# Another order of loads, projection quarters, branches and residuals around the fusions, and other banks

## The reference

```python
# layer 0: attention by heads of 8 channels
q, k, v = x @ wq.T, x @ wk.T, x @ wv.T            # per pixel
pw = pointwise(depthwise5x5(concat(q, k, v)))
out = relu_linear_attention(concat(q, k, v, pw))   # 1024 channels
y = proj(out) * inv + (bn_beta - bn_mean * inv)    # batch norm folded
x2 = y + x
# layer 1: edge maps
sobel, lap, diag, grad = four 3x3 gradient maps of x2
feat = gelu(bn(einsum('kbchw,koc->kbohw', E, w_branch) + b_branch))   # 4 x 128 channels
att = sigmoid(gelu(mean(feat) @ w_att1.T + b_att1) @ w_att2.T + b_att2)
z = w_fuse @ (feat * att) + b_fuse
out = gelu(layernorm_over_channels(z) * ln_gamma + ln_beta) + x2
```

## Time and profile before

| | |
|---|---|
| median of 3 runs | 5199.48 us (5190.54 to 5200.01) |
| profiled execution, its own time | 5196.7 us |
| its span | 5194.8 us |
| mean granted TensorE clock | 0.976 |
| PE busy | 4887.5 us, 94% |
| DVE busy | 2583.4 us, 50% |
| ACT busy | 2021.1 us, 39% |
| `edges` begins / its first projection matmul | 3141.4 / 3157.5 us |

### The profile page before, as it was taken

One profiled execution on the slowest core, in us unless ns is written; L12 is line 12 of the kernel. 1 busy time (PEld: TensorE's weight loads), 2 busy tenths in 40 slices (PEclk: granted clock), 3 DMA queues, 4 the chain that ended last, 5 costly groups with the idle time before them and its releaser, 6 DMA issues. The chain is left out here.

```text
span 5194.8 us, 65292 instructions
## 1 busy us (share of the span) xinstructions
PE 4887.5 (94%) x22760; PEld 3445.3 (66%) x22760; DVE 2583.4 (50%) x3635; ACT 2021.1 (39%) x3671; POOL 1223.1 (24%) x1030
## 2 busy tenths in 40 slices
PE   8999999999999999999999996899899989998958
PEld 7887887888888888888888883344344434443423
DVE  3333333333334334424434421786688578847865
ACT  3333333333333333333323320454555455545555
POOL 2342342342342332332332330000300020011003
PEclk9999999999999999999999998999999999999969
DMA  6666665666666666666656644443344344434313
GB/s 188 198 208 202 197 214 199 198 212 205 198 216 202 204 206 206 206 197 215 206 186 225 203 151 168 142 155 112 130 136 150 108 144 130 141 118 135 117 35 115
DMA packets 390811, 893.09 MB, mean 172 GB/s; under 512 B 33488, under 2 KB 66512, under 8 KB 388240
## 3 DMA queue, kind: packets, MB, share of 16 engines
q1 hardware_dynamic: 390544, 889.18, 51.8%
HBM read 588.74 MB, written 300.32 MB: 171 GB/s over the span
## 5 line engine op out<-in xcount | busy, mean ns | idle before, releaser
L733 POOL TENSOR_TENSOR toeplitz<-taps 128x512 f32<-128x512 f32 x768 | 889.1, 1185 | 955.2 <-PE bank L441 955.2
L441 PEld LDWEIGHTS bank<-toeplitz,columns 128*128 128x128 f32 x8192 | 954.4, 192 | 13.9
L441 PE MATMUL bank<-toeplitz,columns 128*128 128x128 f32 x8192 | 955.7, 275 | 0.0
L1029 PE MATMUL bank<-att,w_proj 128*128 128x512 f32 x2048 | 909.6, 598 | 34.1 <-DVE centred L1314 23.8
L1029 PEld LDWEIGHTS bank<-att,w_proj 128*128 128x128 f32 x2048 | 393.0, 192 | 531.8 <-issue 523.3
L356 PE MATMUL bank<-x_hi,w_hi 128*128 128x512 f32 x1536 | 610.9, 398 | 18.4 <-DVE x_lo L600 18.4
L1362 POOL TENSOR_TENSOR centred<-centred,x_out 128x512 f32<-128x512 f32 x128 | 164.5, 1318 | 1937.1 <-ACT centred L1176 1937.1
L358 PE MATMUL bank<-x_lo,w_hi 128*128 128x512 f32 x1536 | 601.2, 391 | 0.0
L357 PE MATMUL bank<-x_hi,w_lo 128*128 128x512 f32 x1536 | 599.7, 390 | 0.0
L1042 PE MATMUL bank<-edge,w_branch 128*128 128x512 f32 x1024 | 494.5, 629 | 96.1 <-ACT edge L1130 96.1
L671 DVE TENSOR_SCALAR ckey_t<-bank 128x256 f32<-128x256 f32 x256 | 107.4, 419 | 881.8 <-PE bank L441 881.4
(11 more groups left out here) (115 smaller groups left out, 5629.8 us busy)
## 6 DMA issues: line engine op xcount, KB each, us to landing
x_sb<-in_x_tiled SPq DMA_DIRECT2D x128, 1024.0 KB, 6.4
tiles_dram<-tiles SPq DMA_DIRECT2D x128, 867.0 KB, 6.8
loaded<-tiles_dram SPq DMA_DIRECT2D x256, 433.5 KB, 4.0
inverse<-inverse_dram SPq DMA_DIRECT2D x256, 256.0 KB, 5.0
att_dram<-out_sb SPq DMA_DIRECT2D x256, 256.0 KB, 4.1
att<-att_dram SPq DMA_DIRECT2D x64, 1024.0 KB, 6.3
xb<-x_dram SPq DMA_DIRECT2D x128, 330.0 KB, 3.2
x_out<-in_x_pad SPq DMA_DIRECT2D x32, 1056.0 KB, 5.5
```

The source lines that it names most:

```text
L441: last = nc.tensor.matmul(bank[:, v * M:(v + 1) * M], columns[:, h % 2, t - T_K, v + b, a * HT:(a + TO) * HT], w[:, t, d, :], start=(d == ...
L733: last = nc.gpsimd.tensor_tensor(toeplitz[:, h % 2, t, :].rearrange("p (d o r) -> p d o r", o=HD, r=PL), tap, point, ALU.mult)
L1029: last = nc.tensor.matmul(P_BANKS[m][:, :], w_proj[:, i * HALF + k, m * P:(m + 1) * P], att[:, i, k, :], start=(i == 0 and k == 0), stop=( ...
```

## The change

In `edges`:

1. SyncE first loads the mixed weights and the first chunk of `att`, then `edge_vec`, then the first residual, and only then the other constants. VectorE's start waits for `edge_vec` alone.
2. What VectorE makes of the other constants (`constants`), and the four tiny matmuls that average `b_fuse` (`bias_mean`), move behind the three steps of projection alone, into `drain(0, None)`; so do ScalarE's waits for them.
3. `drain` on SyncE loads both halves of `att` for chunk 3 before it writes chunk 2 of x2.
4. In a fresh step TensorE runs q0 q1 b0 q2 b1 q3 b2 b3. In a leaving step it runs q0 b0 q1 b1 q2 b2 b3 q3.
5. `P_BANKS` and `Z_BANKS` are reassigned: the last tile of a fusion lies in bank 4, which is now m = 3 of the projection; banks 5, 6, 7 (m = 0, 1, 2) held tiles of chunk 6. The fresh step's wait for `normed` is split: m = 0 to 2 wait for chunk 6's tiles, m = 3 and b0 for the last. `NORMED` is a larger starting count.
6. VectorE adds the residual of the leaving chunk's m = 2, 3 after `pooled`, not before.

```diff
@@ edges(): banks and the offset of normed
-        P_BANKS, VAR_BANK = banks[4:8], banks[0]
-        Z_BANKS = [banks[i] for i in (4, 5, 6, 7, 1, 2, 3)]
+        VAR_BANK, Z_BANKS = banks[0], banks[1:8]
+        P_BANKS = (banks[5], banks[6], banks[7], banks[4])
+        NORMED = START + KT
@@ SyncE, start and step
-                    for dst, src in ((vec[:, :, :].rearrange("p v m -> p (v m)"), io["vec"]),
-                                     (w_branch[:, :, :, :].rearrange("p k e o -> p (k e o)"), io["branchT"]),
+                    for i in range(2):
+                        load_mixed(0, i)
+                        load_att(0, 0, i)
+                    sp.dma_start(vec[:, :, :].rearrange("p v m -> p (v m)"), io["vec"]).then_inc(vec_loaded, 16)
+
+                def load_constants():
+                    for dst, src in ((w_branch[:, :, :, :].rearrange("p k e o -> p (k e o)"), io["branchT"]),
...
-                    for i in range(2):
-                        load_mixed(0, i)
-                        load_att(0, 0, i)
...
                         load_x(*pj, slot)
+                        if mj is None and prev_p is None:
+                            load_constants()
@@ SyncE, drain
                     if p is not None:
-                        write_x2(p, LAG - 1, (LAG - 1) % 2)
                         sp.wait_ge(att_used, chunk(p, LAG))
                         load_att(p, LAG, 0)
                         sp.wait_ge(projected, KT * chunk(p, LAG))
                         load_att(p, LAG, 1)
+                        write_x2(p, LAG - 1, (LAG - 1) % 2)
                         load_rows(p, 0, 0, 16 * chunk(p, LAG))
@@ TensorE: the mean of b_fuse moves from start into bias_mean, into VAR_BANK
+                def bias_mean():
                     pe.wait_ge(ready, 2)
                     for k in range(KT):
-                        last = nc.tensor.matmul(banks[4][:, 0:1], mean_w[:, :], v("b_fuse")[:, k:k + 1],
+                        last = nc.tensor.matmul(VAR_BANK[:, 0:1], mean_w[:, :], v("b_fuse")[:, k:k + 1],
...
                     pe.wait_ge(ready, 5)
@@ TensorE, project and step
                         if i == 0:
                             pe.wait_ge(summed, KT * c + m + 1)
+                            if fresh:
+                                pe.wait_ge(normed, NORMED + KT * chunk(p, 0) - (KT if m < KT - 1 else 0))
...
-                    if fresh:
-                        pe.wait_ge(normed, START + KT * chunk(pj[0], 0))
-                        pe.wait_ge(std_ready, START + chunk(pj[0], 0))
-                    for k in range(KT):
-                        if pj is not None:
-                            project(*pj, k)
-                        if mj is not None:
-                            branch(*mj, k)
+                    leaving = pj is not None and mj is not None and isinstance(pj[1], int) and pj[1] == LAG - 1
+                    for k in range(KT + 1):
+                        if pj is not None and k < KT and not (leaving and k == KT - 1):
+                            project(*pj, k, fresh)
+                        if mj is not None and k - fresh in range(KT):
+                            if fresh and k == 1:
+                                pe.wait_ge(normed, NORMED + KT * chunk(pj[0], 0))
+                                pe.wait_ge(std_ready, START + chunk(pj[0], 0))
+                            branch(*mj, k - fresh)
+                    if leaving:
+                        project(*pj, KT - 1, False)
 
                 def drain(p, b):
-                    pass
+                    if b is None:
+                        bias_mean()
@@ ScalarE: its waits for scaled and ready move from start to drain(0, None)
-                    act.wait_ge(scaled, 3)
-                    act.wait_ge(ready, 5)
...
@@ VectorE, start: waits for edge_vec alone; the rest of the constants moves
-                    dve.wait_ge(const_loaded, 96)
+                    dve.wait_ge(vec_loaded, 16)
...
+                    dve.wait_ge(scaled, 3)
+
+                def constants():
+                    dve.wait_ge(const_loaded, 80)
                     nc.vector.tensor_scalar(bn_scale[:, :], v("bn1_gamma"), float((1.0 + EPS_BN) ** -0.5), None,
...
@@ VectorE, drain and fusion
                 def drain(p, b):
-                    if p is not None:
+                    if b is None:
                         add_residual(p, LAG - 1, (LAG - 1) % 2, (2, 3))
+                        constants()
...
                     nc.vector.tensor_scalar(pooled[:, :], row_sum[:, :], 1.0 / N, None, ALU.mult).then_inc(pooled_ready, 1)
+                    if not last_image:
+                        add_residual(b + 1, LAG - 1, (LAG - 1) % 2, (2, 3))
                     dve.wait_ge(gate_ready, KT * (b + 1))
```

More of the change, by code:

```diff
@@ L1015, in start, with project @@
                     pe.wait_ge(ready, 5)
-                def project(p, j, quarter):
+                def project(p, j, quarter, fresh):
                     c = chunk(p, j)
@@ L1154, in drain @@
                 def drain(p, b):
-                    if b is not None:
+                    if b is None:
+                        act.wait_ge(scaled, 3)
+                        act.wait_ge(ready, 5)
+                    else:
                         features(b, NCH - 1)
@@ L1229, in start @@
                     dve.wait_ge(mean_ready, 1)
-                    nc.vector.tensor_scalar(z_shift[:, :], v("b_fuse"), banks[4][:, 0:1], None, ALU.subtract).then_inc(ready, 1)
+                    nc.vector.tensor_scalar(z_shift[:, :], v("b_fuse"), VAR_BANK[:, 0:1], None, ALU.subtract).then_inc(ready, 1)
                     nc.vector.tensor_reduce(row_sum[:, :], w_fuse[:, :, :], AX_X, ALU.add).then_inc(ready, 1)
```

12 lines of the change are left out of this document (7 added, 5 removed).

## The result

| | before | changed |
|---|---|---|
| median, in the same session | 5199.48 us (5 runs) | 5169.13 us (5166.08 to 5172.72, 5 runs) |
| ratio | | 0.9948, 95% interval 0.9935 to 0.9961 |
| span of the profiled execution | 5194.8 us | 5164.3 us |
| from attention's last matmul to the end | 2081.2 us | 2054.6 us |

The kernel is 30.3 us faster by the medians; 41.2 had been forecast.

A forecast was written before the change was run, and what follows sets the result against it. PE was taken to set the pace (busy 94%), so only its idle or half-clock time could be saved. Terms 8.0 + 0.3 + 20.4 - 1.5 + 14.0 = 41.2 us off 5196.7 gave 5155; forecast 5147 to 5163, 8-in-10 range 5142 to 5176.

The forecast's parts named there:

- The start: First loads: issuing PE's two loads ahead of the constants starts projection earlier, 8.0 us saved (7.0 to 9.0).
- After the projection-only steps: Before the first b0: the first map decides, not the 8.81 us wait for att; 0.3 us saved (-2.6 to +2.3).
- The leaving step: Three transitions: q3 covers the 3.66 us wait, plus 1.0 us less half clock; 4.7 us each, 14.0 in all.
- b3 of a leaving step: Sign against the forecast: a 4 us wait for maps there would take away what q3 covers.
- The fresh step: Four fresh steps: one quarter less from b0 to next b0, partly lost to a wait; 5.1 us each, 20.4 in all.
- wait of 2.9 us: Before the b0 following a fresh step: VectorE's chain leaves this wait in place of 0.93 us.
- The half clock: Fresh b0 after the fusion, three times: longer idleness costs 0.5 us each (0 to 1), -1.5 us in the sum.
- the freed banks: After the fusion: q0 and q1 run at once, but b0 still comes with its map, so the 8.02 us bring nothing.
- The 11 us of wait before b0: Sign in images two to four: PE's idleness after the fusion falls in one piece before the fresh b0.
- (a): Rival: VectorE paces the shortened steps, so the fresh steps bring nothing; 20.8 us saved, 5176; chance 0.12.
- (b): Rival: the start isn't held by the queue order, so its 8.0 us go; 5163.5; chance 0.08.
- (d): Rival: PE stays at half clock through each fresh step after idleness, 22.3 us a step, 89 for four; 5245; chance 0.03.

The follow-up runs named there:

- start_old: Changed kernel with SyncE's first loads in the order of before; 43.5 us from attention's end to first projection (changed 36.6), 2058.3 us after attention (changed 2054.6).
- leaving_old: Changed kernel with the leaving step's q3 back ahead of b3 and VectorE's residual back ahead of pooled; 2067.6 us after attention, 13.0 longer.
- residual_late: Changed kernel with VectorE's residual for the previous chunk's m = 2, 3 behind the second input tile's maps; 2055.7 us after attention against 2054.6.
- fresh_old: Changed kernel with the fresh step back in order q0 b0 q1 b1 q2 b2 q3 b3; median 5175.99 us, ratio to before 0.9964.
- wait_late: Changed kernel, new banks kept, but a fresh step's q0 and q1 wait for all norms of the fusion before; median 5162.05 us, ratio 0.9932.
- banks_old: Changed kernel with the banks of before, so a fresh step's q0 waits for the last norm; 2041.0 us after attention, 13.5 less.
- ahead_all: Changed kernel with order q0 q1 b0 q2 b1 q3 b2 b3 in every paired step but the leaving one; median 5147.67 us, ratio 0.9911.

## Why the prediction was right or wrong

The direction and the range (5142 to 5176) held, and so did the sizes of the start and of the leaving step; 5155 was 14 us too low. After attention the gain was 26.6 us where the sum has 41.2. The range held partly by luck: its upper end was kept for VectorE setting the pace, which did not happen, and the time that came instead is half clock. Another 3.8 of the 30.5 us between the two profiled executions lie in `attention`, which the change doesn't touch.

- **The start**, 8.0 us: 7.3 in the trace, 6.9 of it by start_old from the order of the loads. PE began 8.2 us after the first issue (3138.14 to 3146.38 in this trace), I had 7.9.
- **After the projection-only steps**, 0.3 us: -1.0 in the trace (111.1 for 110.2). About 0.5 of it lies in the 192 matmuls ahead (85.57 us for 85.06), the rest behind T; among the kernels with the same order the figure varies by 1.5 us. The reading, that the first map decides and the 8.81 us don't count, held, and so did both estimates of what the queue would do (2.6 us lost by the write, 2.1 regained by the rows).
- **The leaving step**, 14.0 us: 13.1 in the trace, 13.0 by leaving_old. The 3.66 us each were right. The half clock gave back 2.1 us in all for 3.0, and not in the fusion's first 40 matmuls, where I had put it (in the first image 19.87 us for 19.24), but in the small matmuls ahead of them. No b3 of a leaving step waited.
- **The fresh step**, 20.4 us: 17.1 from b0 to b0 (4.3, 3.9, 4.7 and 4.3 for 5.1). Taken without b0's own time it is 4.3 us in every image (38.7 before, 34.4 changed): the quarter of 6.87 less the growth of the wait from 0.93 to 3.49. The step that failed is "But VectorE's work ahead of that b0 gets no shorter ... Behind it come the map itself, ScalarE's absolute, the table load and two roots". I took VectorE's chain through the residual to the diagonal map as the one that ends last. It is ScalarE's, through `features`, which can't start before the maps of input 0 are done; residual_late moved the residual and moved nothing. The kernel before could have told: by my chain its b0 would have come at 3308.3 (the diagonal map's 3304.30 and 4.0 us), and it came at 3311.99. What the chain leaves out is one table load and four gelus. The size came near by luck, since the two chains end within 1 us of each other in the changed order. (With its own wait of 2.9 us for 0.93 the term would have been 4.9.)
- **The half clock**, 1.5 us: this was the largest error, 6.7 us. The part that I priced came out smaller than priced: 0.5 us of loss for each fresh b0 of images two to four, measured 0.1 us for the three together (6.30, 5.40 and 6.53 us for 5.92, 5.74 and 6.48). The step that failed is the "wait of 2.9 us" that the fresh step leaves, priced at 2.9 us and nothing for the clock. At 3.5 us it was followed by a b0 at 6.4 to 6.6 us in three images of the changed kernel, 2.7 us each, 8.2 us in all; fresh_old, with 0.93 us of wait, has 3.70 us in all four.

The terms as measured are 7.3 - 1.0 + 17.1 + 13.1 - 8.2 = 28.3. Of the 1.7 us to the 26.6, 1.6 lie in the last image, whose first two branches without projection took 6.32 and 6.29 us for 5.58 and 5.40.

What the prediction missed beside its sum is what the early q0 and q1 forgo. That the freed banks as such bring nothing (V to E0 26.2 us in every kernel) was right; that letting PE run early is at worst a small loss was wrong. In the kernel before q0 came after 8.0 us of idleness and took the half clock on itself, with time to spare. With two quarters in a row that would have carried PE to b0 without a pause: wait_late and banks_old, in which PE starts later, gain 11.4 and 13.5 us over the change. The 11 us of wait before b0 in images two to four came in the last image alone (11.46). In images two and three q0 itself began 5.2 us late, and 3.6 and 4.1 us were left before b0.

Of the rivals, (a) did not happen: in an order that leaves no wait before b0 VectorE still kept pace (ahead_all). (b) fell with start_old. (d) had the right mechanism in miniature: half clock at the branches after idleness, for one branch and not a step. The rule drawn from the Trainium skill, page "ScalarE: Activation LUTs", section "Rules for kernel authors", about 2.7 us per switch of table set, is not what the trace shows: from the end of the activation ahead of a switch to the start of the one behind it there are 1.30 us (3289.90 to 3291.20 above), 1.28 of them the load. The Trainium skill's page "TensorE: Matmul & The Clock Gate", section "HAM oscillation — how this bites in real kernels", says that a matmul kernel which waits between bursts pays the transition to half clock again and again. The slow fresh b0 after 3.25 us of wait and more, in every kernel here, agrees with it; the next b0 after its 3.48 us was slow in some images and not in others. Here the payment falls on whatever PE runs first afterwards, which may or may not be on the path: on q0 and q1 in wait_late, on b0 in the changed kernel.

## What to carry to other kernels

Before freeing an engine to start early, ask what it will wait for next: if that is fixed by others, the early work only moves the idle time, and idle time of PE directly ahead of work on the critical path can cost that work its clock (for a branch here after waits of 3.25 us and more, never after 1.7 us and less). Better idle first, run slow where there is slack, and arrive without a pause. Where a step of cover is taken away before a matmul, follow every engine's queue back from it, not the busiest one's, and then give the cover in pieces as long as the chains need: two quarters or three tiles before b0 and one or two tiles between the others, together with the later start, was worth 28 us over the change by the medians of two sessions, 31 us in the part after attention.

## What the runs showed of the hardware

- A wait of 3.48 us before the b0 that follows a fresh step had different consequences in like places: the matmuls after it took 3.70 us (changed kernel, first image; banks_old, first and last image; and others), 5.40 us, or 6.4 to 6.6 us. Waits of 0.92 us were never followed by anything but 3.70 us. What decides among the three was not settled.
- In images two and three q0 of the fresh step started 5.15 and 5.22 us after the variance matmul though nothing in the profile held it ("issue" above); in the last image it had no such gap (the 11.46 us before b0 are the whole idle time). The seven kernels whose q0 doesn't wait for the last norm all have it there, 4.92 to 5.44 us, and none of them in the last image. The two are where the loop over images jumps back. I didn't test the cause; in the kernel before, the 8.02 us wait hid it.
- The 0.92 us of wait before b0 in the loop go with the place of a table load. There ScalarE loads the table for `features` only once b3 has released it (3417.07, after 3.83 us of idleness). In the steps behind the loop the same load begins at 3455.62 and is over 2.4 us before b3 ends, the gelus follow b3 at once (3459.36), and the next b0 has no wait. No run here moves that load by itself.
- `attention`, identical in all kernels, ended between 3109.75 and 3123.9 us after the span's start, which is half of this change's effect.
